# A gated recurrence with a per-head norm: the weight is multiplied in before the norm instead of after it

## The reference

```python
C = qk * D                                   # D: decays from the gates
normalizer = maximum(abs(C.sum(-1)), exp(-max_log_D))
h = einsum(C / (normalizer + EPS), vh)       # per head
hn = (h - h.mean(-1)) / sqrt(h.var(-1) + LN_EPS)
hn = hn * out_w.reshape(nh, dh)
x = x + hn
```

## Time and profile before

| | |
|---|---|
| median of 3 executions | 2060.69 us (2054.0 to 2062.22) |
| the profiled execution | 2060.8 us |
| its span, first to last instruction | 2058.9 us |
| recurrence, 128 chunks, in the span | about 58 to 1185 us |
| routing, experts and output stage | about 1185 to 2059 us |
| PE busy in the span | 82% |
| DVE, POOL, ACT busy | 67%, 65%, 53% |

### The profile page before, as it was taken

How to read it: one execution, slowest core, us unless ns; L and a number is a source line. 1 busy time by engine, 2 the same in 40 slices (tenths; PEclk the granted TensorE clock), 3 DMA queues, 4 the chain that set the end, 5 groups by cost and what they waited for, 6 DMA issues and landing times. The chain is left out here.

```text
span 2058.9 us, 59080 instructions
## 1 busy us (share of the span) xinstructions
PE 1686.7 (82%) x22734; PEld 1281.1 (62%) x22893; DVE 1386.4 (67%) x2971; ACT 1083.1 (53%) x2499; POOL 1347.7 (65%) x1306
## 2 busy tenths in 40 slices
PE   4898988898989898898989715999957869596893
PEld 3777777777777777777777514999953334242341
DVE  2577767777777877677777783333444859589597
ACT  3676767777777767676776500222214344343442
POOL 1567666676767676667667703776733869699698
PEclk9999999999999999999999955999988989798897
DMA  5122222222222223222220105454532547556475
GB/s 191 60 89 88 94 94 80 93 95 94 94 95 94 94 79 95 94 93 90 85 79 33 48 3 231 137 142 136 142 106 51 147 113 173 124 128 153 105 172 119
DMA packets 106598, 218.04 MB, mean 106 GB/s; under 512 B 13008, under 2 KB 14416, under 8 KB 105552
## 3 DMA queue, kind: packets, MB, share of 16 engines
q1 hardware_dynamic: 96080, 180.68, 30.6%
q0 software_dynamic: 10240, 33.56, 5.6%
HBM read 147.08 MB, written 67.11 MB: 104 GB/s over the span
## 5 line engine op out<-in xcount | busy, mean ns | idle before, releaser
L318 POOL TENSOR_TENSOR rec_hn<-rec_hn,rec_out_w 128x512 f32<-128x512 f32 x128 | 199.4, 1558 | 213.1 <-DVE rec_hn L739 213.1
L1409 PE MATMUL out_z_ps<-out_ao,out_hot 32*128 32x512 f32 x2048 | 240.2, 618 | 32.9 <-DVE out_z_half L1477 22.8
L296 POOL TENSOR_TENSOR rec_hrs<-rec_harg,rec_minus_half 128x8 f32<-128x8 f32 x128 | 213.1, 1664 | 10.0
L1315 POOL TENSOR_TENSOR out_x_half<-out_x_half,out_ln_b 128x512 f32<-128x512 f32 x128 | 163.0, 1307 | 79.7 <-DVE out_z_half L1477 79.7
L1409 PEld LDWEIGHTS out_z_ps<-out_ao,out_hot 32*128 32x128 f32 x2048 | 107.1, 194 | 163.7 <-issue 133.7
L1112 ACT ACTIVATE exp_rows_t<-exp_t_ps 128x512 f32<-128x512 f32 x128 | 69.5, 594 | 245.7 <-PE exp_t_ps L1080 245.7
L705 DVE TENSOR_TENSOR rec_c<-rec_s_ps,rec_d 128x512 f32<-128x512 f32 x256 | 165.0, 686 | 38.0 <-PE rec_s_ps L426 34.9
L1355 ACT ACTIVATE out_z_half<-out_z_half,out_rs 128x512 f32<-128x512 f32 x128 | 82.0, 711 | 195.0 <-POOL out_rs L1319 194.1
L536 ACT ACTIVATE rec_d<-rec_l_ps 128x512 f32<-128x512 f32 x256 | 151.7, 593 | 62.3 <-PE rec_l_ps L450 61.6
L1325 POOL TENSOR_TENSOR out_x_half<-out_x_half,out_z_half 128x512 f32<-128x512 f32 x128 | 164.7, 1318 | 24.2 <-ACT out_z_half L1355 24.2
L1092 PE MATMUL exp_q_ps<-exp_wqkv,exp_rows_t 128*128 128x192 f32 x1024 | 178.1, 328 | 0.0
(11 more groups left out here) (215 smaller groups left out, 4387.6 us busy)
## 6 DMA issues: line engine op xcount, KB each, us to landing
rec_x_ring<-in_x SPq DMA_DIRECT2D x128, 256.0 KB, 2.9
rec_ctx_ring<-in_ctx SPq DMA_DIRECT2D x128, 256.0 KB, 3.0
x_scratch<-rec_x_ring SPq DMA_DIRECT2D x128, 256.0 KB, 2.0
out_x_half<-x_scratch SPq DMA_DIRECT2D x128, 256.0 KB, 5.6
out<-out_x_half SPq DMA_DIRECT2D x128, 256.0 KB, 4.0
exp_wqkv<-in_wqkv SPq DMA_DIRECT2D x4, 1536.0 KB, 17.6
exp_x_rows<-x_scratch,rowid POOLq DMA_INDIRECT x128, 3.5
out_wo<-in_wo SPq DMA_DIRECT2D x1, 2048.0 KB, 7.9
```

The costliest lines, as they stand in the source:

```text
L296: nc.gpsimd.tensor_tensor(hrs[:, G % 2], harg[:, G % 2], mhalf[:], ALU.pow).then_inc(hrs_done, 1)
L318: nc.gpsimd.tensor_tensor(h, h, w8[:], ALU.mult).then_inc(hw_done, 1)
L1315: nc.gpsimd.tensor_tensor(xt[H % XR][:, q, :], xt[H % XR][:, q, :], lb[:], ALU.add).then_inc(xb_done, 1)
L1409: mm = nc.tensor.matmul(z_ps[r][:], hot[B % 2][g, hp, m * P:(m + 1) * P], ao[B % 2][g, hp, :], start=(hp == 0), stop=(hp == HP - 1))
```

## The change

`out_weights` of chunk g-1 now runs in step g, ahead of `head_scales` of the same chunk. It reads the numerators as soon as ACT has copied them out of PSUM, multiplies them by the weights, and writes into two new buffers, `rec_num_w0` and `rec_num_w1`. `head_norm` reads these instead of the numerators, and `residual` waits for `head_norm`, which is on its own engine, instead of for POOL. The place of `num` in its ring is free when `out_weights` has read it. No instruction is added or removed. Lines behind the new buffer move by one to three, so L318 is L319 in the changed kernel, L739 is L741 and L759 is L761.

```diff
+    nw = [sb(f"num_w{i}", [P, NH, DH]) for i in range(2)]
...
         def out_weights(G):
-            h = hn[G % 2][:].rearrange("p h d -> p (h d)")
-            pool.wait_ge(hn_done, G + 1)
-            nc.gpsimd.tensor_tensor(h, h, w8[:], ALU.mult).then_inc(hw_done, 1)
+            pool.wait_ge(o_read, 2 * G + 2)
+            after(pool, hn_done, G - 1)
+            nc.gpsimd.tensor_tensor(nw[G % 2][:], num[:, G % NR, :, 0:DH], w8[:].rearrange("p (h d) -> p h d", h=NH),
+                                    ALU.mult).then_inc(nw_done, 1)
...
-            if valid(g - 2):
-                out_weights(g - 2)
             if valid(g - 1):
+                out_weights(g - 1)
                 head_scales(g - 1)
...
         def numerators(g):
             act.wait_ge(o_full, g + 1)
             if g >= NR:
-                act.wait_ge(hn_done, g - NR + 1)
+                act.wait_ge(nw_done, g - NR + 1)
...
         def head_norm(G):
             dve.wait_ge(hrs_done, G + 1)
             after(dve, x1_done, G - 1)
-            vec.tensor_tensor(hn[G % 2][:], num[:, G % NR, :, 0:DH],
+            dve.wait_ge(nw_done, G + 1)
+            vec.tensor_tensor(hn[G % 2][:], nw[G % 2][:],
                               hrs[:, G % 2].unsqueeze(2).broadcast_to([P, NH, DH]), ALU.mult).then_inc(hn_done, 1)
...
         def residual(G):
             x1 = xr[:, G % XR, :]
-            dve.wait_ge(hw_done, G + 1)
+            dve.wait_ge(hn_done, G + 1)
```

More of the change, by code:

```diff
@@ L191, in recurrence_stage @@
     ssum_done, harg_done = sem("ssum_done"), sem("harg_done")
-    hrs_done, hn_done, hw_done, x1_done = sem("hrs_done"), sem("hn_done"), sem("hw_done"), sem("x1_done")
+    hrs_done, hn_done, nw_done, x1_done = sem("hrs_done"), sem("hn_done"), sem("nw_done"), sem("x1_done")
     y_link, y_var, y_ve, y_rs = sem("y_link"), sem("y_var"), sem("y_ve_done"), sem("y_rs")
```

## The result

| | before | after |
|---|---|---|
| median of 11 executions | 2060.69 us (2052.78 to 2062.72) | 2067.39 us (2062.58 to 2072.37) |
| the profiled execution, its span | 2060.8, 2058.9 us | 2066.45, 2064.6 us |

The ratio after to before is 1.0039, with a 95% interval of 1.0025 to 1.0054. The kernel became slightly slower, by less than the 0.5% that the prediction took as its bound. It forecast 2073.2 us with a range of 2056 to 2091; the range holds the result, and the forecast's own range of 2068 to 2078 misses it by 0.6 us. The prediction had put 58% on slower by more than 0.5% and 34% on within 0.5%, so the less likely of the two came.

A forecast was written before the change was run, and what follows sets the result against it. PE's own order was taken to bound the kernel, busy 1000 of the recurrence's 1127 us. PE's lateness, +14.3 us, and the drain, -1.9, summed to +12.4 on 2060.8: 2073.2 us, range 2056 to 2091, the forecast's own 2068 to 2078.

The forecast's parts named there:

- The drain, -1.9 us: Last chunk: residual begins right after rec_hn, 1.28 us, and the scale before it starts earlier, 0.64 us.
- The product, 1.27 us: POOL's product in its new place takes 1.27 us, with 1.04 and 1.66 as the other prices considered.
- `peaks`, 0.81 late: DVE in step 41: peaks, held off by the product, ends at 424.35 in place of 423.54.
- `values` 0.39 late: POOL's values of step 42 starts 0.39 us later, behind the late sum, rec_harg and power.
- The residual, 0.73 late: DVE in step 42: held off by the product, the residual ends at 430.95 in place of 430.22.
- PE, 0.51 late, 28 times, +14.3 us: PE's L472 waits for the second rec_c in step 42, 0.51 us late, in 28 cycles: 14.3 us.
- Steps with 0, 1 and 3: nothing: In steps 41, 43 and 44 delays cost nothing; DVE's idle time and a 0.36 us ACT margin absorb them.
- The sum, +12.4 us: Whole kernel: +14.3 for PE's lateness less 1.9 for the drain, on 2060.8 us, giving 2073.2 us.
- rival 2: Fewer low clock stretches in steps g mod 4 = 3, 1.5 us each: 2059.7 us with the collision, 2045.4 without; 8%.
- Rival 1: In step 42 the product doesn't catch the residual, with products of about 1.0 us; only the drain remains, 2058.9 us; 20%.
- Rival 3: PE's new idle stretch brings low clock in up to all 28 cycles, up to 28 us on top, 2102; 12%.
- rival 4: The product takes 1.66 us, or step 44 loses its margin: up to 2103 us; 5%.

The follow-up runs named there:

- the product waits in all steps: Changed kernel, with POOL's product also waiting for head_norm of chunk g-2 in every step: 2057.77 us, ratio 0.9998.
- the second comparison: Changed kernel and kernel before run again unaltered: 2066.41 us, ratio 1.0039, for the changed one; 2054.35 us in one execution for the kernel before.
- the runs with the exchange: ACT's parts(n, 1) put ahead of put_ctx in steps g mod 4 = 3: kernel before 2003.64 us, changed kernel 2016.78, changed with wait in all steps 2003.62.
- the one with two products: Changed kernel with the product of steps g mod 4 = 2 issued twice into the same buffer: 2068.65 us, ratio 1.0061.
- the kernel with the wait back in step 2 alone: Changed kernel, with the product waiting for head_norm only in steps g mod 4 = 2: 2064.43 us, ratio 1.0043.

## Why the prediction was right, and where its terms were off

The direction, the place and the count of the cost were forecast and are shown by experiment. That the time lies within the range is in part luck: the cost came nearly in full, and the clock, which the forecast had left out of its sum, took about a third of it back.

- **What bounds the kernel: right.** PE's busy time is unchanged. The time that POOL won is idle again one instruction later. The only gain that reached anything is in the drain.
- **The drain, -1.9 us.** From the start of the last step to the end of the last residual it is 13.98 us before and 11.73 after, 2.25 less, in both executions of each kernel, where 1.9 were forecast. From there to the next stage the DMA of constants decides, and it let through 1.2 to 2.0.
- **The product, 1.27 us: mis-sized.** It takes 1.19 us, also in the steps where L318 took 1.66, since it no longer runs with L712. The bounds of 1.04 and 1.66 held. The Trainium skill, "GPSIMD Engine Reference", section "Elementwise — side-by-side cycle accounting", led to an estimate of 1.12 us and a sum of +4 us. The measured row lies midway between it and the row of the same shape that the forecast took.
- **`peaks`, 0.81 late:** 0.73 at the median, that is, 0.08 less, as the product is. `values` 0.39 late: 0.37.
- **The residual, 0.73 late:** 0.63 in step 42, 0.62 at the median. It takes 0.91 us and not the 1.0 or more that were named as a sign, since it begins later against a shorter product.
- **PE, 0.51 late, 28 times, +14.3 us:** 0.46 in step 42, and +12.6 and +12.0 us over all steps of the kind. The product's price enters the walk twice, in step 41 and in step 42. So with 1.19 in it the residual would be 0.57 and PE 0.35 late, 28 x 0.35 = 9.8, and the price alone does not carry the difference. Two small terms run the other way. POOL starts on the sum 0.15 us after its end (425.23 + 0.67 = 425.90 to 426.05), and not after the 0.08 taken from another hand-over. And L473's second half, once it has waited, takes 0.05 us longer (0.51 in place of 0.46). That the total came so near 14.3 is thus errors that cancel in part. The new wait was to show near 14 us and shows 7.4: the view counts the idle time ahead of the first half alone, 0.26 us in step 42. L473 is 0.13 longer, and the 0.07 by which it overlapped with the matmuls ahead of it are gone as well.
- **Steps with 0, 1 and 3: nothing.** Wrong by a little. Steps with 1 grew by 2.2 us, in a few single ones such as step 21 (9.38 to 9.92), where L483 idles 0.78 us in place of 0.23 with no releaser that the profile names. They lie 28 steps apart: 21, 49, 77 and 105. It is there without the low clock too, and in steps 49 and 105 also where the product waits in all steps (9.61 and 9.77 us), so the collision is not needed for it. Its cause wasn't tried and stays open.
- **The sum, +12.4 us:** the profiled execution shows +5.7, the medians +6.7 here and +8.6 in the second comparison. The step that failed is the assumption that the clock stays as it was. The prediction had it as rival 2, at 8%, with 1.5 us for each low stretch. It came in part, beside the forecast: 6 and 7 low stretches in place of 9 and 8. In the two profiled executions of the first comparison that is 3 x 1.5 = 4.5 of the 4.7 us that the steps with 3 took less. Over all executions it is 2.6 stretches and 3.9 us, as estimated above. That the collision costs 12 to 13 us is shown by the runs with the exchange, that the low stretches cost time by their absence there. Why they become fewer is not shown. The two kernels whose steps 2 take 8.52 us without the exchange (the changed one and the one with two products) have mean clocks of 0.9325 to 0.9333; the kernel with the wait back in step 2 alone has longer cycles too, but 0.930. No run varies the idle time of step 42 by itself.

Rival 1 (the product doesn't catch the residual) had its point of decision wrong. A product shorter by x ends 2x sooner, and DVE stands ready x sooner. By the prediction's own walk, 430.40 - 2x meets 429.92 - x at 0.48 us less, a product of 0.79 and not of about 1.0. At about 1.0 the residual is still caught, only PE no longer waits. At 1.05 us it takes 0.77 us, and the step is 0.18 us longer than before, where the walk gives 0.07. Rival 3 did not occur, and of rival 4 neither part did.

## What to carry to other kernels

An instruction that waits has a place in time as well as a cost. Take the wait away, and the work runs against other neighbours: here POOL's product moved from behind `head_norm`, where nothing that PE waits for was reading, onto the two-operand instructions ahead of `rec_c`. Before moving work between DVE and POOL, list the two-SBUF-operand instructions of DVE that fall into its new place, and follow those that stand ahead of what PE waits for. And ask first what the bound engine waits for in each cycle: PE's 41.6 us for one small instruction of POOL were worth 54 us, POOL's own 213 us of idle time none that can be measured.

## What the runs showed of the chip

- A DVE instruction of 512 elements that is held off ends 0.54 to 0.56 us after POOL's (the residual of step 42: 430.68 against 430.12), one of 8 elements 0.02 after (`peaks`, 424.10 against 424.08). What it costs is thus POOL's remaining time, and for the long one about 0.1 us less.
- DVE is served between two products of POOL that follow each other (the residual ends at 432.10, the first product at 431.56, and the second takes 1.51 us). And the power L297 on 8 elements, 1.64 us from 435.30, does not hold off the residual that starts inside it at 435.94 and takes its usual 0.66. The Trainium skill, "SBUF — State Buffer", section "SBUF: two separate sides", says that whichever of the two starts first gets the shared ports for the whole instruction. The product agrees (residual 0.91 us), the power does not: it had long started.
- The same product takes 1.19 us with two full operands into a new buffer, 1.05 with one of them repeated, and took 1.27 in place.
- In the recurrence, behind its first step, the clock was low only in steps with g mod 4 = 3, where PE idles for 1.4 us ahead of L408 (L407 before). Without this wait it stayed at 1.00, and each low stretch was worth 1.5 us on top of the wait itself.
